# Value products inside a third, one mask per unit of scores, kept rows in 4 KB pieces, and the last group's sums on TensorE, in a fused attention and expert layer

## What is computed

```
x = x + layernorm(attention(layernorm(x)))   # 16 heads of 16 channels, rotary, causal
x = x + layernorm(ffn(layernorm(x)))
ffn(h) = h + sum over 4 chosen of 16 experts of gate * (silu(h Wg) * (h Wu)) Wd
           + (silu(h Ws_g) * (h Ws_u)) Ws_d  # shared expert
```

## Time and profile before

| what | value |
|---|---|
| median of 3 runs | 1130.15 us (1129.67 to 1133.27) |
| profiled execution, its own time | 1136.02 us |
| its span | 1134.2 us |
| PE busy, records | 886.7 us (78%), 7044 |
| DVE busy | 679.0 us (60%) |
| ACT busy | 448.6 us (40%) |
| POOL busy | 440.0 us (39%) |
| mean granted PE clock | 0.844 of full speed |
| DMA moved | 168.78 MB, mean 149 GB/s |

### The profile page before, as it was taken

One profiled execution on the slowest core, in us unless ns is written; L12 is line 12 of the kernel. 1 busy time (PEld: TensorE's weight loads), 2 busy tenths in 40 slices (PEclk: granted clock), 3 DMA queues, 4 the chain that ended last, 5 costly groups with the idle time before them and its releaser, 6 DMA issues.

```text
span 1134.2 us, 21559 instructions
## 1 busy us (share of the span) xinstructions
PE 886.7 (78%) x7044; PEld 651.4 (57%) x7044; DVE 679.0 (60%) x1918; ACT 448.6 (40%) x756; POOL 440.0 (39%) x422
## 2 busy tenths in 40 slices
PE   4369798887987997888886798695987699988810
PEld 3245465664654665655564555584875588877700
DVE  4467658677668578577476475552652233677737
ACT  2115444444343444443442445342542355444400
POOL 4422113125316316306313114454555545555642
PEclk9659898897798698798696789898998999988955
DMA  3684716217226235324465322343544555987764
GB/s 131 149 228 106 215 39 168 67 36 216 73 53 176 85 76 163 103 76 115 118 228 178 106 73 93 112 149 105 158 138 159 169 164 166 362 303 260 243 243 149
DMA packets 101467, 168.78 MB, mean 149 GB/s; under 512 B 14704, under 2 KB 73072, under 8 KB 101104
## 3 DMA queue, kind: packets, MB, share of 16 engines
q1 hardware_dynamic: 87536, 128.85, 39.7%
q0 software_dynamic: 13824, 38.55, 9.0%
HBM read 90.15 MB, written 76.68 MB: 147 GB/s over the span
## 4 chain that ended last, share of the span: by engine, by line
PE 46%; DVE 17%; issue 11%; SPq 8%; DMA 7%; ACT 6%; POOL 3%; another core or an unknown queue 2%; ACTq 0%; DVEq 0%; POOLq 0%
PE ring L1444 6%; PE ring L1316 6%; PE ring L1250 5%; PE ring L1251 4%; PE ring L1252 4%; PE ring L1287 4%; PE ring L1302 4%; ACT prob L1180 3%; DVE nmax L778 3%; DMA xg<-sorted_rows 3%; PE ring L1465 3%; SPq L581 2%; PE ring L1264 2%; PE ring L1430 2%
## 5 line engine op out<-in xcount | busy, mean ns | idle before, releaser
L778 DVE TENSOR_REDUCE nmax<-ring 128x2 f32<-128x1024 f32 (+3 forms) x256 | 201.2, 818 | 103.8 <-PE ring L1293 87.3
L1180 ACT ACTIVATE prob<-ring 128x1024 f32<-128x1024 f32 (+1 forms) x192 | 164.1, 879 | 217.4 <-PE ring L1307 195.8
L688 POOL DMA_INDIRECT expert_rows<-ys,dest x160 | 157.1, 982 | 139.3 <-ACT ys L1134 80.5
L680 POOL DMA_INDIRECT sorted_rows<-xr,idx_all x128 | 127.5, 996 | 86.9 <-DVE xr L937 53.7
L1444 PE MATMUL ring<-we,xh 128*128 x640 | 159.8, 395 | 0.0
L1287 PE MATMUL ring<-k_st,q_st 48*128 48x512 f32 (+3 forms) x512 | 116.0, 460 | 42.4 <-ACT prob L1180 35.6
L1302 PE MATMUL ring<-q_st,k_st 50*128 50x384 f32 (+3 forms) x512 | 109.3, 445 | 34.0 <-DMA q_st<-mrow 10.8
L1444 PEld LDWEIGHTS ring<-we,xh 128*128 128x128 f32 x640 | 121.6, 200 | 14.4
L1000 DVE SCALAR_TENSOR_TENSOR sl<-sl,got,ring 128x128 f32<-128x128 f32 x160 | 48.4, 344 | 123.1 <-ACT sl L1232 88.3
L1316 PE MATMUL ring<-prob,v_sb 128*32 128x512 f32 (+3 forms) x1024 | 111.6, 539 | 0.8 <-ACT prob L1180 0.4
L658 POOL TENSOR_TENSOR rot<-rot 128x512 f32<-128x512 f32 x16 | 20.4, 1273 | 222.5 <-DVE rot L770 222.5
(11 more groups left out here) (192 smaller groups left out, 1672.3 us busy)
## 6 DMA issues: line engine op xcount, KB each, us to landing
xg<-sorted_rows SPq DMA_DIRECT2D x160, 134.0 KB
parts<-part SPq DMA_DIRECT2D x32, 512.0 KB
ykt<-expert_rows SPq DMA_DIRECT2D x16, 1024.0 KB
k_st<-parts SPq DMA_DIRECT2D x64, 128.0 KB
q_st<-parts SPq DMA_DIRECT2D x64, 128.0 KB
we<-w_exp SPq DMA_DIRECT2D x1, 6144.0 KB, 20.0
sorted_rows<-zeros SPq DMA_DIRECT2D x2, 2144.0 KB, 10.5
sorted_rows<-zeros SPq DMA_DIRECT2D x32, 134.0 KB
```

What stands on the lines that cost most here:

```text
L680: pool.indirect_dma_start(out=xs[group_of(s)], out_offset=bass.IndirectOffsetOnAxis(ap=idx_all[:, s, t, k:k + 1], axis=0), in_=xr[:, s % 2 ...
L688: pool.indirect_dma_start(out=yk, out_offset=bass.IndirectOffsetOnAxis(ap=dest[:, j % 8, b:b + 1], axis=0), in_=ys[:, j % NYS, b, :], in_o ...
L778: dve.tensor_reduce(nmax[:, Q % 2, :, pp, qb], slot[:, :, col:col + (qb + 1) * P], AX.X, ALU.max, negate=True).then_inc(s_max, 1)
L1180: act_e.activation(prob[:, u % 2, 2 * half:2 * half + 2, 0:width], slot[:, :, 0:width], ACT.Exp, scale=SCALE).then_inc(s_exp, 1)
```

## The change

It has four parts.

- The due time of AV goes from 1.4 to 1.15 after the start of its third: a third is then ST, S, AV, ST, S, and the other steps. ACT's copy to `o_t` moves with it, ahead of the exponentials of the second ST.
- The four mask products of a unit are issued once for all its parts, with an access pattern that repeats the mask over the parts' diagonal blocks. In S units they come last as before, in ST units they now come first, and the ST products accumulate on them.
- x1 and z are stored and loaded in the layout `packed`: a partition's four rows lie together in DRAM, in a piece of 4 KB.
- For sequences 5 to 7 PE sums the four result rows: four fp32 products of 512 columns with the identity as weights, accumulated in ring pair 2, whose two banks alternate. DVE adds z to this total in one step. POOL's first sum is gone. For sequences 0 to 4 DVE's adds stay, with another count of semaphore steps.

```diff
-            add(3 * Q + 7 + m + 1.4, "AV", Q, m)
+            add(3 * Q + 7 + m + 1.15, "AV", Q, m)
...
+        def packed(t):
+
+            return t.rearrange("(p t) d -> p t d", p=P)
+
+        def sums_before(s, h):
+
+            n = 2 * s + h
+            alone = min(n, 2 * SHARED)
+            return 4 * alone + n - alone
...
-                sp.dma_start(rows(x1_dram[s]), x1[:, :, :]).then_inc(s_x1st, 16)
+                sp.dma_start(packed(x1_dram[s]), x1[:, :, :]).then_inc(s_x1st, 16)
...
-                sp.dma_start(rows(z_dram[s]), z[:, :, :]).then_inc(s_zst, 16)
+                sp.dma_start(packed(z_dram[s]), z[:, :, :]).then_inc(s_zst, 16)
...
-                sp.dma_start(zt[:, s % 2, :, :], rows(z_dram[s])).then_inc(s_cz[s % 2], 16)
-                sp.dma_start(x1t[:, s % 2, :, :], rows(x1_dram[s])).then_inc(s_cz[s % 2], 16)
+                sp.dma_start(zt[:, s % 2, :, :], packed(z_dram[s])).then_inc(s_cz[s % 2], 16)
+                sp.dma_start(x1t[:, s % 2, :, :], packed(x1_dram[s])).then_inc(s_cz[s % 2], 16)
...
-            def first_sum(s, h):
-
-                pool.wait_ge(s_cl[2 * (s % 2) + h], 16 * (s // 2 + 1))
-                y = ykt[:, s % 2, NHALF * h:NHALF * h + NHALF, :, :]
-                pool.tensor_tensor(y[:, :, 0, :], y[:, :, 0, :], y[:, :, 1, :], ALU.add).then_inc(s_cp, 1)
...
-                elif kind == "CA" and st[2] >= SHARED:
-                    first_sum(st[2], st[3])
                 elif kind == "CS":
                     final_rstd(st[2], st[3])
...
             def final_sums(s, h):
                 tiles = slice(NHALF * h, NHALF * h + NHALF)
                 y = ykt[:, s % 2, tiles, :, :]
-                done = 3 * (2 * s + h)
+                done = sums_before(s, h)
+                if s >= SHARED:
+                    if h == 0:
+                        dve.wait_ge(s_cz[s % 2], 32 * (s // 2 + 1))
+                    n = 2 * (s - SHARED) + h
+                    dve.wait_ge(s_cp, n + 1)
+                    total = ring[2][:, n % 2, :].rearrange("p (t d) -> p t d", t=NHALF)
+                    dve.tensor_tensor(y[:, :, 0, :], total, zt[:, s % 2, tiles, :], ALU.add).then_inc(s_cs, 1)
+                    return
...
                 dve.wait_ge(s_cl[2 * (s % 2) + h], 16 * (s // 2 + 1))
                 dve.tensor_tensor(y[:, :, 2, :], y[:, :, 2, :], y[:, :, 3, :], ALU.add).then_inc(s_cs, 1)
-                if s < SHARED:
-                    dve.tensor_tensor(y[:, :, 0, :], y[:, :, 0, :], y[:, :, 1, :], ALU.add).then_inc(s_cp, 1)
+                dve.tensor_tensor(y[:, :, 0, :], y[:, :, 0, :], y[:, :, 1, :], ALU.add).then_inc(s_cs, 1)
...
                 if h == 0:
                     dve.wait_ge(s_cz[s % 2], 32 * (s // 2 + 1))
                 dve.wait_ge(s_cs, done + 1)
                 dve.tensor_tensor(y[:, :, 2, :], y[:, :, 2, :], zt[:, s % 2, tiles, :], ALU.add).then_inc(s_cs, 1)
-                dve.wait_ge(s_cs, done + 2)
-                dve.wait_ge(s_cp, 2 * s + h + 1)
+                dve.wait_ge(s_cs, done + 3)
                 dve.tensor_tensor(y[:, :, 0, :], y[:, :, 0, :], y[:, :, 2, :], ALU.add).then_inc(s_cs, 1)
...
-                dve.wait_ge(s_cs, 3 * (2 * s + h + 1))
+                dve.wait_ge(s_cs, sums_before(s, h) + (1 if s >= SHARED else 4))
...
+            def blocks_of(bank, parts):
+
+                first, step = parts[0], (parts[1] - parts[0] if len(parts) > 1 else 1)
+                return bank.rearrange("p (n c) -> p n c", c=P)[:, first:first + step * (len(parts) - 1) + 1:step, :]
...
             def score_unit(Q, pp, m, slot):
-                for qb, col in S_PARTS[m]:
+
+                parts = S_PARTS[m]
+                for n, (qb, col) in enumerate(parts):
                     q0, width = qb * P, (qb + 1) * P
                     for par in range(2):
                         r = slice(64 * par, 64 * par + SROWS)
                         pe.matmul(slot[:, par, col:col + width], q_st[r, Q % NQ, pp, q0:q0 + P], k_st[r, Q % NQ, pp, 0:width],
-                                  start=True, stop=False, skip_group_check=True)
-                    c0 = col + qb * P
-                    for h in range(2):
-                        for par in range(2):
-                            r = slice(64 * par, 64 * par + 64)
-                            last = pe.matmul(slot[:, par, c0 + 64 * h:c0 + P], halves_b[r, h, :], mask_b[r, h, 64 * h:P],
-                                             start=False, stop=True, skip_group_check=True)
+                                  start=n == 0, stop=False, skip_group_check=True)
+                diagonal = [col // P + qb for qb, col in parts]
+                for h in range(2):
+                    for par in range(2):
+                        r = slice(64 * par, 64 * par + 64)
+                        mask = mask_b[r, h, 64 * h:P].unsqueeze(1).to_broadcast([64, len(parts), P - 64 * h])
+                        last = pe.matmul(blocks_of(slot[:, par, :], diagonal)[:, :, 64 * h:P], halves_b[r, h, :], mask,
+                                         start=False, stop=True, skip_group_check=True)
                 last.then_inc(s_S, 1)
...
             def transposed_unit(Q, half, m, slot):
-                for kb, col in ST_PARTS[m]:
+
+                parts = ST_PARTS[m]
+                diagonal = [col // P for kb, col in parts]
+                for h in range(2):
+                    for par in range(2):
+                        r = slice(64 * par, 64 * par + 64)
+                        mask = maskt_b[r, h, 0:64 * (h + 1)].unsqueeze(1).to_broadcast([64, len(parts), 64 * (h + 1)])
+                        pe.matmul(blocks_of(slot[:, par, :], diagonal)[:, :, 0:64 * (h + 1)], halves_b[r, h, :], mask,
+                                  start=h == 0, stop=False, skip_group_check=True)
+                for kb, col in parts:
                     k0, width = kb * P, T - kb * P
                     for par in range(2):
                         r = slice(64 * par, 64 * par + MROWS)
-                        pe.matmul(slot[:, par, col:col + width], k_st[r, Q % NQ, half, k0:k0 + P], q_st[r, Q % NQ, half, k0:T],
-                                  start=True, stop=False, skip_group_check=True)
-                    for h in range(2):
-                        for par in range(2):
-                            r = slice(64 * par, 64 * par + 64)
-                            last = pe.matmul(slot[:, par, col:col + 64 * (h + 1)], halves_b[r, h, :],
-                                             maskt_b[r, h, 0:64 * (h + 1)], start=False, stop=True, skip_group_check=True)
+                        last = pe.matmul(slot[:, par, col:col + width], k_st[r, Q % NQ, half, k0:k0 + P],
+                                         q_st[r, Q % NQ, half, k0:T], start=False, stop=True, skip_group_check=True)
                 last.then_inc(s_ST, 1)
...
+            def sum_results(s, h):
+
+                n = 2 * (s - SHARED) + h
+                pe.wait_ge(s_cl[2 * (s % 2) + h], 16 * (s // 2 + 1))
+                if n == 0:
+                    pe.wait_ge(*free_of(RING_LAST[2]))
+                elif n >= 2:
+                    pe.wait_ge(s_cs, sums_before(s - 1, h) + 1)
+                for k in range(TOPK):
+                    last = pe.matmul(ring[2][:, n % 2, :], ident, ykt[:, s % 2, NHALF * h:NHALF * h + NHALF, k, :],
+                                     start=k == 0, stop=k == TOPK - 1)
+                last.then_inc(s_cp, 1)
...
+                elif kind == "CA" and st[2] >= SHARED:
+                    sum_results(st[2], st[3])
```

More of the change, by code:

```diff
@@ L460, in block_kernel @@
         s_cz = [sem(f"residuals_back{i}") for i in range(2)]
-        s_cp = sem("first_sums")
+        s_cp = sem("results_summed")
         s_cs = sem("final_sums")
```

## The result

The changed kernel takes 1099.62 us (median of 4 runs, 1096.73 to 1104.94), the kernel before 1131.71 us beside it: a ratio of 0.972, 95% interval 0.968 to 0.976. The forecast was 1124 with a range from 1110 to 1139. The direction was right, the size and the range were not: 32 us came off, not 6.5.

The account below looks back on a forecast made before the run. It took TensorE's work and waits to bound attention, and VectorE the tail. Attention's -27 + 13 + 8 - 5 = -11, times 0.8, gave -9; tail +3, kept rows -0.5: -6.5, hence 1124 us, range 1110 to 1139.

Parts of the forecast that it names:

- What bounds the kernel now: Attention: TensorE leads the chain; its large wait is score products for exponentials, 35.1 us, mostly before second S units.
- What is late next: Attention after the AV move: new waits, mainly for the second ST's exponentials, 13 us on, bounds 5 and 25.
- 19 bare thirds: Second thirds in attention with no other TensorE work, where the second ST's exponentials would cause 9 us of new wait.
- Breaks: Attention: one more change of product shape in 76 thirds, 0.09 us each, 8 us on, bounds 0 to 14.
- One mask for all parts: Attention's score units: fewer mask instructions with the same columns, 5 us off, bounds 0 to 13.
- The order of ST units: Attention: masks ahead of the ST product change its end by less than 0.1 us, hidden by the exponentials' queue; nothing.
- 0.8 of the total: Attention's -11 us counted as -9, since TensorE is on the chain for a good part, not all, of that stage.
- work +3, waits -14 and clock 0: Attention's terms: breaks +8 and masks -5; removed waits -27 and new waits +13; no change of clock.
- The clock: Rival: fewer pauses raise attention's granted clock from 0.84 to 0.88, 15 to 20 us more, 1107 us; chance 0.15.
- The tail: After the last matmul: TensorE's sums, with the last waiting on SP's transfer chain, end 2.9 us later; 3 on.
- Kept rows: Stores and loads in 4 KB pieces, mostly hidden behind the transfers' slack: 0.5 us off.
- The slower rival: Attention: first S units wait for second exponentials as often as second S units did before; about 1139 us, chance 0.22.

Follow-up runs that it names:

- e7: The kernel before, run again unchanged for its profile on this chip: 1122.36 us, ratio 0.998.
- e10: The kernel before with only AV moved to 1.15: 1117.21 us, ratio 0.990 to the kernel before.
- e8: The changed kernel with AV back at 1.4: 1122.49 us, ratio 0.997 to the kernel before.
- e5: The changed kernel once more, beside the kernel before on the same chip: 1092.8 us, ratio 0.970.
- e11: The kernel before with only the changed score units (merged masks, in ST units ahead of the products): 1124.1 us, ratio 0.994.
- e9: The changed kernel again, as measure for the runs beside it: 1100.41 us, ratio 0.973 to the kernel before.
- e12: The changed kernel with the ST units' merged masks behind the products: 1101.83 us, ratio 0.975 to the kernel before.
- e14: The changed kernel with one mask group per part again, in ST units all ahead of the products: 1050.55 us, ratio 0.982 to the kernel before.
- e16: The changed kernel again, where the kernel before took 1070.41 us: 1043.61 us, ratio 0.978.
- e13: The changed kernel with AV at 1.25, a third being ST, S, ST, AV, S: 1073.76 us, ratio 1.004 to the kernel before.
- e3: The kernel before with only the last group's sums moved to TensorE: 1074.96 us, ratio 1.005.
- e4: The kernel before with only the kept rows in 4 KB pieces: 1067.46 us, ratio 1.000.
- e15: The changed kernel with the result rows of (7,1) queued ahead of sequence 7's kept rows: 1037.06 us, ratio 0.971 to the kernel before.

## Why the prediction was wrong

Three steps failed. The order of masks and products in ST units was put at nothing and saved 14 to 16 us of TensorE's work. Row maxima got no wait and became the largest one. And the parts were added up, with TensorE's clock left as it was, where they needed each other and the low clock came to cost 12 to 34 us less. One by one:

*What bounds the kernel now.* Right as far as it went: the wait for exponentials was real, stood before second S units, and the moved AV took half of it away (38.1 to 18.9 us, e7 to e10, forecast 35 to about 15). What is left stands mostly before second S units still (12 waits, 10.8 us in e10), not before first ones as forecast.

*What is late next.* Here the first step failed. The prediction named the second ST's exponentials in 19 bare thirds and allowed 9 us for them; in e10 first S units waited three times, 4.8 us, 3.8 of it at one place. It gave nothing for row maxima, and these became the large new wait: 10.7 us in e7, 26.1 in e10, 31 to 36 with AV moved and masks changed. The working weighed only ACT's side of the ring; VectorE's side, with maxima up to 1.23 us for an S unit plus rotary and router work, was named nowhere. Net idle of the AV move was -3.5 us (e7 to e10, two chips), forecast -27 + 13; the scatter of single profiles is nearly as large as that difference.

*Breaks.* The rows read right: S masks to AV take 0.19 us in the changed kernel too (169.19 to 169.38), as do S masks to a step of other shape (171.62 to 171.81). So a change of shape costs 0.09 us more here. But the work grew by only 2.6 us from e7 to e10, which is the spread of profiles with the same attention, and by 2 to 6 with the changed masks (e8 to e5, e11 to e9), not by 8; the bounds, 0 to 14, hold it. By the Trainium skill (TensorEngine Tiling (Array Packing), Key Properties) a changed tiling mode drains TensorE; the rows with 0.19 against 0.10 us agree; the total, a few us at most, shows that the rule alone prices nothing.

*One mask for all parts.* The term most wrong in size: 5 us with bounds 0 to 13, measured 24 to 27 us of work (447.1 to 420.3 from e7 to e11, 449.7 to 426.0 from e10 to e9). It has two halves. Merging and joining the parts gives 9 to 10 (449.7 to 440.1 from e10 to e12, 434.0 to 424.7 from e14 to e16), twice the forecast and inside its bounds. The order of ST units, masks ahead of the products, was put "at nothing", and gives 14 to 16 (440.1 to 426.0 from e12 to e9, 449.7 to 434.0 from e10 to e14): the S products now follow ST products instead of masks, 0.12 us sooner by the two timelines above (0.62 against 0.50 us). There are 178 such pairs, two in each third that has both kinds, so 14 to 16 us are some 0.08 us for each. A sign of it could have been read before: the S products of 384 columns ahead of the masks at 162.32 start at 162.06, and their columns take 0.16 of these 0.26 us; 0.10 is something else. The sum asked how many instructions go, not how many changes of kind.

*The terms are no sum.* This is the main fault. The working added work, waits and breaks and took 0.8 of the total. The runs show 1.0% and 0.6% alone, and 2.7% together, with the tail's loss of 0.5% already in it. Saved work was worth little (e11 0.6%; e8 0.3%, with the sums' loss in it) while the S units ran into exponentials. For attention the sum had work +3, waits -14 and clock 0; the first two profiles show work -21, idle +16 and clock -28, and e7 to e5 on one chip -23, +14 and -12. So its signs of work and of idle time were both wrong. What was missing is a timeline of a third with both changes in it.

*The clock.* The sum gave it nothing. It had stood as a rival with 0.15 and 15 to 20 us, and 1107 us, the nearest of all to the result; its condition, a granted mean of 0.88 in attention instead of 0.84, is what the first two profiles show. In the profiles of the slower kind the low clock costs 84 to 89 us before and 55 to 72 after, so 12 to 34 us lie there, as much as in any term. The reason given, fewer pauses, does not fit: TensorE waited 88 times in attention before and 85 times after, and its idle time rose. What raised the clock no run isolates: e12 and e9 have more idle than before and a higher clock, e13 has an idle time near e9's and a lower one. That stays open.

*The tail.* The best part. Forecast 2.9 us later, measured 3.9 in the profile (45.4 to 41.5) and 0.5% alone in e3. Steps: VectorE's half every 3.4 us (1067.56 to 1071.07 is 3.51), store of (5,1) 16.5 us after the first arrival (measured 16.8), the transfer chain as the bound with TensorE idle before the last sum. The last sum started 28.8 us after the arrival, not 26.2: 0.3 us from the store's issue, 0.7 from the store, which took 2.8 us to land against 2.1, and the rest from the transfer of the result rows, 8.3 us from issue to the sum against the 7.0 read before (0.4 of gain had been taken off that). Timeline of SP's queue and of that sum, against the earlier trace rows:

```profile
1074.47 0.38 SPq L617 DMA_DIRECT2D out<-zt  x1
1077.30 0.33 SPq L599 DMA_DIRECT2D zt<-z_rows  x1
...
1078.15 0.43 SPq L612 DMA_DIRECT2D ykt<-expert_rows  x1
```

```profile
1086.50 5.40 PE L1379 MATMUL ring<-ykt,kc 128*128 128x512 f32 x8 [4.51 <-DMA ykt<-expert_rows]
```

*Kept rows.* 0.5 us off and in truth nothing that can be measured (e4), though 12,288 packets went. The 13% between the two rates in the earlier trace rows did not become time. The Trainium skill (DMA: Bandwidth & Descriptors, Specifications) gives line rate from 512 B, by which 1 KB pieces lose nothing; e4's ratio of 1.000 agrees with it.

*The slower rival* (waits as many as before) had a true core: idle time in attention did not fall, it rose, from 95 to 111 us. But it was the row maxima, not the second exponentials, that took the place of the old wait. Less work and a higher clock made the kernel faster all the same.

## What to carry to other kernels

On a bound made of a ring of buffers, price a saving and a removed wait together, since each alone gave 0.6 and 1.0% here and both 2.7%: draw one period with both, find which engine releases each slot, and ask it of every engine that reads the ring, not of the one that waits most. Count orderings as well as instructions: the order of masks and products alone was 14 to 16 us of work here, more than the merging. Where a transfer chain bounds the end, try its order on the queue first; here that gave 0.6% (e15), and faster sums had lost 0.5% (e3). And no count of idle time forecast the clock.

## What the runs showed of the hardware

The same program took 1068 and 1070 us on two chips and 1122 to 1132 on others, with no difference of its instructions. Some 31 to 36 us of it lie in the expert stretch, whose code the parts do not touch (first to last transpose, 308.2 us in e4, 338.9 in e7, 344.6 in the first profile). The ratio of the whole change stayed between 0.970 and 0.978 on all of them.

Merged masks of twice the columns (64x256) cost 0.27 us to the next step of another shape (173.01 to 173.28 to the AV in the changed kernel's trace), the single ones 0.19: the columns' 0.08 us more.

TensorE came out of idleness in the tail with a first sum of 6.5 us (1057.68 to VectorE's add at 1064.19; forecast 5.5) and middle ones of 3.4. The last sum took 5.4 to 5.8 us in seven profiles and 3.7 in three (e3, e15, e16), between the forecast's 3.5 us at 2.4 GHz and 6.9 at 1.2 GHz; the full 6.9 was met in none. In the first profile (1086.50 to the add at 1091.94) the granted clock was still 1.00 when it began, after 4.5 us of idleness; it fell to 0.50 within the sum, and was back at 1.00 before its end.
